# Layer-0 attention: the gate piece of a group issued behind the loads of V and ahead of the spread of K

## What is computed

```
tp = silu(time_emb) @ Wt + bt                      # one row for each sequence
shift_msa, scale_msa, gate_msa, shift_mlp, scale_mlp, gate_mlp = split(tp, 6)
h = layernorm(x) * (1 + scale_msa) + shift_msa
q, k, v = split(h @ Wqkv + bqkv)                   # 16 heads of 8
attn = softmax(q @ k.T / sqrt(8)) @ v              # 32 x 32 for each sequence and head
x = x + gate_msa * (attn @ Wproj + bproj)
x = x + gate_mlp * mlp(layernorm(x) * (1 + scale_mlp) + shift_mlp)
...                                                # layer 1: RMS norm, one head of 128, MLP
```

## Time and profile before

| what | us |
|---|---|
| median of 3 runs | 254.11 (253.97 to 254.25) |
| the profiled execution | 254.23 |
| its span, first to last instruction | 252.4 |
| TensorE busy | 239.5 (95%) |
| VectorE, ScalarE, GpSimd busy | 162.8, 156.8, 154.2 |
| attention 0, about | 17 to 102 |

### The profile page before, as it was taken

The page is one execution under the profiler, slowest core; times in us unless marked ns, Lnnn a source line. Parts: engine busy times, 40 slices in busy tenths (PEclk is TensorE's granted clock), DMA queues, the critical chain, the costliest instruction groups (busy, mean ns, idle before and its releaser), DMA issues.

```text
span 252.4 us, 9860 instructions
## 1 busy us (share of the span) xinstructions
PE 239.5 (95%) x3727; PEld 181.0 (72%) x3727; DVE 162.8 (65%) x507; ACT 156.8 (62%) x396; POOL 154.2 (61%) x173
## 2 busy tenths in 40 slices
PE   5899879999999989999999999899999999999995
PEld 5676667787877866766778669677775766677775
DVE  7898888988989997455554543578888354442102
ACT  5469867866966849745445666887856666443340
POOL 4486846585685778677656667788784544554120
PEclk9999999999999999999999999999999999999999
DMA  6943334325256222412100000000000011110112
GB/s 192 326 127 91 122 128 116 122 65 164 94 145 206 104 76 71 134 62 75 71 12 0 0 0 0 4 3 4 0 4 0 0 44 42 42 29 14 44 42 83
DMA packets 17163, 18.01 MB, mean 71 GB/s; under 512 B 1648, under 2 KB 12656, under 8 KB 17136
## 3 DMA queue, kind: packets, MB, share of 16 engines
q1 hardware_dynamic: 16272, 15.41, 20.0%
q10 hardware_dynamic: 864, 2.24, 2.8%
HBM read 11.48 MB, written 4.59 MB: 64 GB/s over the span
## 4 chain that ended last, share of the span: by engine, by line
PE 80%; DVE 4%; POOL 4%; issue 4%; DMA 2%; SPq 2%; ACT 2%; POOLq 0%; ACTq 0%; DVEq 0%
PE bank L1275 23%; PE bank L1064 10%; PE pair L1064 10%; PE bank L1032 5%; PE bank L1142 5%; PE pair L1112 4%; PE bank L1124 3%; PE bank L1163 3%; PE pair L1288 3%; PE pair L1079 2%; PE bank L1071 2%; PE bank L1282 2%; PE bank L1313 2%; PE bank L1112 2%; PE bank L1092 2%
## 5 line engine op out<-in xcount | busy, mean ns | idle before, releaser
L818 ACT ACTIVATE xhat<-X,shift,rstd 128x128 f32 (+1 forms) x88 | 36.9, 487 | 41.1 <-POOL shift L340 41.1
L1275 PE MATMUL bank<-W,Kx 128*128 128x128 f32 x512 | 59.6, 275 | 0.0
L1275 PEld LDWEIGHTS bank<-W,Kx 128*128 128x128 f32 x512 | 58.5, 192 | 1.0 <-issue 1.0
L351 POOL TENSOR_TENSOR h<-hA,B 128x512 f32<-128x512 f32 x31 | 32.5, 1048 | 32.6 <-DVE hA L555 32.4
L555 DVE TENSOR_TENSOR hA<-bank,A 128x512 f32<-128x512 f32 x31 | 21.1, 681 | 32.9 <-PE bank L1032 17.7
L1064 PE MATMUL bank<-h,W 128*128 128x512 f32 x62 | 32.0, 597 | 0.1
L338 POOL TENSOR_TENSOR rstd<-v_sb,minus_half 128x4 f32<-128x4 f32 x24 | 24.5, 1020 | 10.9 <-DVE v_sb L540 5.8
L1064 PE MATMUL pair<-h,W 128*128 128x512 f32 x62 | 29.4, 592 | 0.0
L359 POOL TENSOR_TENSOR Ss<-Sc,smax 128x512 f32<-128x512 f32 x16 | 16.8, 1050 | 18.9 <-DVE smax L581 18.8
L896 ACT ACTIVATE Kx<-bank,col 128x512 f32<-128x512 f32 x32 | 21.7, 677 | 8.1 <-PE bank L1064 8.1
L1032 PEld LDWEIGHTS bank<-ident,xhat 128*128 128x128 f32 x124 | 15.0, 142 | 14.8 <-issue 12.9
(11 more groups left out here) (155 smaller groups left out, 467.3 us busy)
## 6 DMA issues: line engine op xcount, KB each, us to landing
values_scratch<-Vs SPq DMA_DIRECT2D x8, 288.0 KB, 2.1
Vx<-values_scratch SPq DMA_DIRECT2D x32, 72.0 KB
gate<-gates_scratch SPq DMA_DIRECT2D x8, 256.0 KB
gate<-gates_scratch SPq DMA_DIRECT2D x4, 512.0 KB
out<-X SPq DMA_DIRECT2D x7, 256.0 KB, 2.3
Kx<-Ks SPq DMA_DIRECT2D x24, 64.0 KB, 2.3
X<-x SPq DMA_DIRECT2D x4, 256.0 KB, 5.5
W<-weights ACTq DMA_DIRECT2D x1, 640.5 KB, 3.8
```

The source lines that it names most:

```text
L351: pool.tensor_tensor(by_seq(h[:, p, :]), by_seq(hA[:, p, :]), B[:, seqs(gg)].unsqueeze(2).broadcast_to([P, GB, L]), ALU.add).then_inc(h_re ...
L818: last = act.activation(xhat[:, p, P * t:P * (t + 1)], X[:, x_tile(gg, t), :], ACT.Identity, bias=shift[:, p, t:t + 1], scale=rstd[:, p, t ...
L1275: last = pe.matmul(y[t // 2][:, P * t:P * (t + 1)], gT[:, p, n, P * t:P * (t + 1)], w(f"W2_{phase // 2}", n), start=(n == 0), stop=(n == N ...
```

## The change

In `spread_v` the call of `spread_gates(0, g, NG)` moves from directly behind the store of V to behind the four loads of V. For group 0 it stood behind the loads already, outside the function; it and its wait are now inside, in the same order.

```diff
                 sp.dma_start(values_d[p], Vs[:, p, :]).then_inc(v_stored[p], 16)
                 if g == 0:
                     store_gates()
-                else:
-                    spread_gates(0, g, NG)
                 sp.wait_ge(v_stored[p], 16 * (g // 2 + 1))
                 wait(sp, pv_done, 2 * g - 2)
                 src = values_d[p].rearrange("(q m) (r f) -> r m q f", q=TB, r=HQ)
                 for r in range(HQ):
                     sp.dma_start(Vx[L * r:L * (r + 1), p, r, :].rearrange("m (q f) -> m q f", q=TB),
                                  src[r]).then_inc(v_spread[p], 16)
+                if g == 0:
+                    sp.wait_ge(gates_stored, 16 * TB)
+                spread_gates(0, g, NG)
 
             sp.wait_ge(zeros_ready, 2)
             spread_v(0, 0)
-            sp.wait_ge(gates_stored, 16 * TB)
-            spread_gates(0, 0, NG)
             for g in range(1, NG):
                 spread_v(g, g % 2)
                 if g < NG - 1:
                     spread_k(g + 1, (g + 1) % 2)
```

## The result

| | before | changed |
|---|---|---|
| median of 5 runs, us | 254.25 | 256.78 |
| ratio, 95% interval | | 1.0101 [1.0072, 1.0131] |
| span of the profiled execution | 252.4 | 254.5 |
| TensorE's waits for K in its rounds of L1142 (now L1141) | 1.2, once | 3.3, five times |

The account below looks back on a forecast made before the run. TensorE, 95% busy, was taken as the bound. A 0.87 us gain in group 1, 0.33 lost in group 6 and 0.1 for groups 4 and 6 gave -0.44 us: 253.7, range 253.2 to 254.1, wider 252.9 to 255.1.

Parts of the forecast that it names:

- What bounds the kernel, and where to look: TensorE, 95% busy, bounds it; the only wait to win is 1.20 us for K of group 2 in `weigh0(1)`.
- Part 1: Group 1's V loads: without the gate piece ahead, the slow second load goes; TensorE waits 0.33 instead of 1.20, gaining 0.87 us.
- the 1.64 us: Extra issue time of group 1's four V loads, 3.37 against 1.73 us in groups 2, 4 and 6; forecast to go whole.
- rival C: Group 1: the second V load's slow issue is not the gate's, so no effect; K lands at 36.5, time 254.4; chance 0.18.
- Part 2: Behind V's loads, the gate piece's transfer delays K on shared engines; hidden in groups 2 to 5, 0.33 us wait in group 6.
- T + 5.37: K's landing, T being the piece's issue: 4.24 to its last data, 0.69 for K, 0.44 from last data to landing.
- 4.24 + 0.69: Behind the piece's issue: 4.24 us until its last data move, then 0.69 us estimated for moving K.
- a cover of 0.07: Groups 4 and 5: K's later landing stays hidden from TensorE's fourth round with only 0.07 us to spare.
- rival A: Slower: the piece holds up K in every group, +2.0 us at worst, +1.0 taken, 255.1; chance 0.22.
- a cover of 0.4: Group 2: K's later landing stays hidden from TensorE's fourth round with 0.4 us to spare.
- The W1 load: Group 6: issued at 82.82 instead of 82.39, delaying ACT to about 85.5; cover 0.1, costed at nothing, 0.5 if it fails.
- The waits that moved, GpSimd's reader and group 0: The piece's waits are already met, GpSimd reads a step of 10 us after issue, group 0 is unchanged: no cost.

Follow-up runs that it names:

- the kernel with the halves: Against the changed kernel, each piece of groups 1 to 7 cut in two, one half behind V's loads, the other behind K's spread: 261.58 us, ratio 1.0293.

## Why the prediction was wrong

The measured 256.78 us lies outside both ranges, 253.2 to 254.1 and the wider 252.9 to 255.1.

**What bounds the kernel, and where to look: right.** Busy times hardly moved (TensorE 240.3 us against 239.5), and the difference is about that of TensorE's waits at the fourth round of `weigh0`.

**Part 1, the step that failed first.** That taking the 0.58 us of issue away frees nothing was right: the first load goes out 2.10 us behind the store, 2.12 before. That the slow second load "does not come back" was wrong. The loads took 2.66 us (3.37 before), so 0.7 of the 1.64 us went, and the piece was issued at 30.68 instead of 29.47 (0.3 of that because the store was later too). K then landed 3.4 us behind its fourth issue instead of 2.0. Without any piece the loads took 2.55, and the wait was 1.2 us all the same. I had set the piece against the slow load because group 1 was the only slow one of four; what set group 1 apart was not the piece alone, which all four had. The trace has an instruction fetch beside its second load, and the kernel with the loop written out shows that fetches do this to groups that were free of it; that they do it in group 1 is the likely cause, and no run took them away. The text named the objection (all four had the piece) and then took the full 1.64 us. Its own rival C had the counter-evidence, two slow issues of K with no piece in transfer, and it was right for group 1, at a chance of 0.18: by its working K lands at 36.5, and it landed at 36.66.

**Part 2, a term mis-sized.** The direction was right: K waits for the piece, and its landing follows the engines and the bytes ahead of it. The term T + 5.37 was too small: 5.84 us in groups 4 and 5, 5.98 in group 1, 6.07 in group 6. The piece's own 2.75 us came from a stretch in which it was alone. In group 4 of the changed kernel data moved until 66.4 us (the engines' share is 0.25 from 66.00 to 66.25, 0.03 in the next quarter, then 0.00), 5.3 us behind the piece's issue at 61.10, where 4.24 + 0.69 gives 4.93: so most of the 0.5 is in moving the piece and K together, and little in the 0.44 behind it. This is the estimate that would have needed a margin, because two groups had a cover of 0.07: with 0.5 more they wait, and they did, 0.46 and 0.25 us. The chance for rival A, "from 0.07 us on in groups 4 and 5", was too low at 0.22, and its price, halved to +1.0, was too: +2.1 in the profiled execution, and +2.5 between the medians. No issue of K stalled behind the piece in groups 4 and 6; the landing alone did it.

**Group 2** had a cover of 0.4 in the working only if nothing else slowed K. There K landed 3.84 us behind its fourth issue, 6.9 us behind the piece; it has the piece and the slow landing of the first groups together (3.2 us in group 2 without any piece); how the two add was not separated. **Group 6** was to lose 0.33 and lost 0.84, by the same 0.5 of part 2.

**The W1 load: right.** It went out at 84.52, ScalarE waited for it 1.8 us instead of 0.6, and TensorE did not wait for ScalarE in the changed kernel. How near that was to costing something is shown by the kernels with the piece behind K.

**The waits that moved, GpSimd's reader and group 0: right;** GpSimd's waits for the gate are of 0.2 to 0.3 us each, as before.

**The sum again,** with what was measured: 0.28 in group 1, 0.26, 0.46, 0.25 and 0.84 in groups 2, 4, 5 and 6, +2.09 us on 252.4, against the -0.44 of the prediction: 1.15 us of the difference is group 1, a gain that was not there and a loss in its place; the rest, 1.4, is the mis-sized landing behind it.

## What to carry to other kernels

A transfer in a DMA queue delayed those behind it by about its whole length on the engines that it used. So ask on how many engines a transfer runs, and not only how many bytes it has: 256 KB on 4 of 16 engines took 2.75 us here, as long as 1 MB would take on all 16 at the same rate for each engine (an estimate). Put such a transfer into a time in which the queue waits anyway and behind which only DMAs with slack follow; here that is the wait for the store of V. And before putting a wait down to a neighbour in the queue, look whether the groups without that wait have the same neighbour.

## What the runs showed of the hardware

- Instruction fetches disturbed transfers: with TensorE's loop written out (26 fetches of 16 KB instead of 17, eight of them from 55 to 90 us, where there had been none) K's landing rose from 1.9 us to 3.0 to 3.4 in the groups that had been free of them, and the issues of V's loads on SP's queue from 1.73 us to 2.5 and more.
- A broadcast read of 256 KB from 4 rows, each repeated 32 times, ran at a share of 0.27 of the DMA engines for 2.75 us. From 16 rows, each repeated 8 times, it ran at 0.49 for about 1.75.
- A small DMA that met a large load of another queue was late: 64 KB of K landed in 4.0 us beside 640 KB of weights, and in 3.7 with the narrow piece behind K, against 1.9 when it went out ahead of that load.
- A wait of TensorE of 2.4 us was followed by a granted clock of 0.57 over 4 us, and one of 2.7 (narrow piece behind K, group 5) by 0.50 over 4.1. Others were not: 2.8 us in the kernel with the halves and the second wait of 2.8 us with the loop written out were followed by 1.00.
